# Two units of the FFN inside attention's last steps, expert 1's split moved to ScalarE and VectorE, zero rows issued by SyncE

## What is computed

```python
x = x + layernorm(attn(layernorm(x)))     # x: 2 batches x 2048 tokens x 256
x = x + layernorm(ffn(layernorm(x)))
# attn: 16 heads of 16, feature map elu(x)+1 on q (scaled) and k, gate = sigmoid(x Wg' + bg), per token
#   S = g * S + k v' ; y = q S ; output y Wo'
# ffn: one shared SwiGLU of width 512 for all tokens, and 8 experts of the same shape, top 2 per token:
swiglu = lambda x, w1, w2, w3: (silu(x @ w1) * (x @ w2)) @ w3
out = sum_e w[e] * swiglu(x, ew1[e], ew2[e], ew3[e]) + swiglu(x, sw1, sw2, sw3)
```

## Time and profile before

| | us |
|---|---|
| median of 3 runs | 824.59 |
| all runs | 824.56, 824.59, 828.3 |
| the profiled execution | 819.94 |
| its span, first to last instruction | 818.0 |
| TensorE busy | 725.9 (89%) |
| VectorE busy | 558.4 (68%) |
| GpSimd busy | 506.5 (62%) |
| ScalarE busy | 457.2 (56%) |
| mean granted TensorE clock | 0.964 |

### The profile page before, as it was taken

One profiled execution on the slowest core, in us unless ns is written; L12 is line 12 of the kernel. 1 busy time (PEld: TensorE's weight loads), 2 busy tenths in 40 slices (PEclk: granted clock), 3 DMA queues, 4 the chain that ended last, 5 costly groups with the idle time before them and its releaser, 6 DMA issues.

```text
span 818.0 us, 25456 instructions
## 1 busy us (share of the span) xinstructions
PE 725.9 (89%) x8863; PEld 607.8 (74%) x8863; DVE 558.4 (68%) x1126; ACT 457.2 (56%) x1023; POOL 506.5 (62%) x725
## 2 busy tenths in 40 slices
PE   4888989898999987287887999999999999999984
PEld 4667767786777776275776999999999986688873
DVE  4898897998998897478665444344444434358996
ACT  2655666575566654222444666656565657545443
POOL 4133334878687777578964888866666544316664
PEclk9999999999999998698999999999999999999998
DMA  7324332445344343956441111122222222227984
GB/s 256 95 76 128 107 93 80 138 126 152 101 144 119 107 132 102 311 165 195 120 128 51 46 54 40 55 72 79 87 86 82 70 60 66 85 89 208 187 177 89
DMA packets 57481, 93.25 MB, mean 114 GB/s; under 512 B 7216, under 2 KB 35760, under 8 KB 57360
## 3 DMA queue, kind: packets, MB, share of 16 engines
q1 hardware_dynamic: 40512, 60.66, 25.7%
q0 software_dynamic: 10672, 22.57, 10.2%
q10 hardware_dynamic: 6176, 8.40, 3.6%
HBM read 59.60 MB, written 32.01 MB: 112 GB/s over the span
## 4 chain that ended last, share of the span: by engine, by line
PE 40%; DVE 8%; POOL 7%; issue 5%; DMA 2%; ACT 2%; DVEq 0%; POOLq 0%; ACTq 0%; SPq 0%
PE bank L1294 22%; PE bank L1338 12%; PE bank L1314 3%; POOL xs_scratch L555 3%; PE bank L1278 2%; DVE wpart L1559 1%; POOL xs_scratch L588 1%; DVE bank L1655 1%; POOL W L1728 1%; DVE W L850 1%; DVE wtmp_p L1609 1%; DVE stc L1622 1%; DMA W<-gate_scratch 1%; DVE gl L1646 1%; ACT gh L1380 1%
## 5 line engine op out<-in xcount | busy, mean ns | idle before, releaser
L1294 PE MATMUL bank<-xh,W 128*128 128x256 f16 x1504 | 263.5, 277 | 21.2 <-DVE gl L1646 15.7
L1294 PE MATMUL bank<-xl,W 128*128 128x256 f16 x752 | 207.9, 277 | 1.4 <-issue 1.4
L1294 PEld LDWEIGHTS bank<-xh,W 128*128 (+1 forms) x1504 | 149.2, 99 | 45.9 <-issue 16.0
L1380 ACT ACTIVATE gh<-bank 128x512 f16<-128x512 f32 x103 | 61.3, 595 | 159.2 <-DVE bank L1655 146.4
L1338 PE MATMUL bank<-W,gh 128*128 (+1 forms) x824 | 138.0, 273 | 0.8 <-DVE gl L1646 0.8
L1743 POOL DMA_INDIRECT yt_scratch<-ysh,dest x71 | 76.2, 1073 | 97.7 <-ACT ysh L1435 58.5
L1646 DVE TENSOR_TENSOR gl<-bank,gh 128x512 f16<-128x512 f32 x103 | 71.0, 689 | 68.7 <-ACT gh L1380 67.4
L1338 PE MATMUL bank<-W,gl 128*128 (+1 forms) x412 | 112.3, 273 | 0.0
L555 POOL DMA_INDIRECT xs_scratch<-xn_all,posi x64 | 87.5, 1367 | 27.5 <-issue 15.2
L1655 DVE SCALAR_TENSOR_TENSOR bank<-sl,w_scale,bank 128x512 f32<-128x512 f32 x94 | 70.9, 755 | 48.7 <-PE bank L1294 40.2
L607 PE MATMUL bank<-xnT,wT 128*128 128x256 f32 x384 | 94.1, 397 | 2.3 <-ACT xnT L369 2.3
(11 more groups left out here) (205 smaller groups left out, 1386.4 us busy)
## 6 DMA issues: line engine op xcount, KB each, us to landing
W<-gate_scratch SPq DMA_DIRECT2D x64, 256.0 KB, 4.1
ysh<-yt_scratch SPq DMA_DIRECT2D x16, 512.0 KB, 4.7
xt<-xs_scratch SPq DMA_DIRECT2D x31, 260.0 KB
W<-in_L_ffn_ew_dram ACTq DMA_DIRECT2D x15, 512.0 KB, 3.8
W<-in_L_ffn_ew_dram SPq DMA_DIRECT2D x9, 512.0 KB, 8.7
x_in<-in_L_attn_x_dram SPq DMA_DIRECT2D x16, 256.0 KB, 3.7
out_dram<-x SPq DMA_DIRECT2D x16, 256.0 KB
xT_scratch<-xn2T SPq DMA_DIRECT2D x16, 256.0 KB
```

Of the source, the lines that this page charges most:

```text
L1294: last = mm(dst[n % 2][:, i * R:(i + 1) * R], W16[:, e, m, s, at:at + P], a[:, k, :], start=(k == 0 and s == 0 and a is x_h), stop=(k == K ...
L1380: act.activation(gh[t.u % 2][h][:, :], (pH1 if t.kind == "single" else pH2)[n % 2][:, :], ACT.Copy)\
```

## The change

Phase B's functions become generators that stop at `yield`; phase A's functions get `first_units`, a call that runs phase B up to its next `yield`, and the rest of phase B runs when phase A has ended. So units 0 and 1 are cut into pieces that stand at fixed places of iterations 17 and 18 on ScalarE, VectorE, TensorE and SyncE. What `tensor_b` waited for at its start is now waited for where it is needed.

- TensorE: behind all of iteration 17's work both halves of unit 0 and the first half of unit 1 (72 matmuls), behind iteration 18's (the router of step 15) the second half of unit 1; the two projections after phase A.
- Expert 1's three matrices are split as the shared ones are, by ScalarE (`scaled`, `high`) and VectorE (`low`) in iterations 17 and 18; `pool_b` begins with expert 2.
- The zero rows are eight plain DMAs of 128 rows by SyncE (`pad_experts`), each at a row read into a register, in phase B between the loads of units 3 and 4.
- `beside` is spread anew: searches for experts 2 and 3 in units 1 and 2, the table's last turn in unit 3, gap 2; the 15 searches for experts 4 to 8 in gaps 0 and 2 of units 4 to 11; the last scales in unit 12, gap 1. SHARE, the units at which SyncE shares maxima, goes from (0, 7) to (2, 11).
- The total of the counts goes to bank 6 (X1) in place of bank 7.

```diff
 def sync_a(sp, first_units):
             for i in range(FIRST, LAST):
+                if i == C + 1:
+                    first_units()
...
 def scalar_a(act, first_units):
                 on(share, i - 5)
+                if i == C + 1:
+                    first_units()
+                    for m in (3,):
+                        scaled(m)
+                        high(m)
+                if i == C + 2:
+                    first_units()
...
                 on(norm_x1, i - 3)
+                if i == C + 2:
+                    first_units()
                 on(turn_y, i - 2)
                 on(values, i - 1)
                 on(turn_xn2, i - 3)
                 on(lambda s: mask_q(s, 1), i - 1)
+                if i == C + 1:
+                    for m in (4, 5):
+                        scaled(m)
+                        high(m)
+                if C + 1 <= i <= C + 2:
+                    first_units()
...
 def pool_a(pool):
-            pool.wait_ge(s_pad, 1)
-            for e in range(E):
-                settle(pool)
-                pool.indirect_dma_start(xs_d[:, :], bass.IndirectOffsetOnAxis(ap=pad_row[:, e:e + 1], axis=0),
-                                        zrow[:, :], None).then_inc(s_padded, 16)
...
 def tensor_a(pe, first_units):
                 on(lambda s: scores(s, 0), i - 1)
-
-            pe.wait_ge(S["kT_ready"], C)
-            mm(X2[:, 0:E], ones[:, :], before[:, :, NB], start=True, stop=True).then_inc(s_total, 1)
+                if C + 1 <= i <= C + 2:
+                    first_units()
+
+            mm(X1[:, 0:E], ones[:, :], before[:, :, NB], start=True, stop=True).then_inc(s_total, 1)
...
 def vector_a(dve, first_units):
+                if i == C + 2:
+                    low(4)
+                    low(5)
+                    first_units()
                 on(stat_x1, i - 3)
+                if i == C + 2:
+                    first_units()
...
                 on(scan, i - 1)
+                if i == C + 1:
+                    first_units()
+                    low(3)
                 on(stat_o, i - 2)
...
 def sync_b(sp):
-        SHARE = (0, 7)
+        SHARE = (2, 11)
+            def pad_experts():
+                sp.wait_ge(s_pad, 1)
+                for e in range(E):
+                    row = sp.value_load(pad_row[0:1, e:e + 1], min_val=0, max_val=ZERO - P)
+                    sp.dma_start(xs_d[bass.ds(row, P), :], zrow[:, :]).then_inc(s_padded, 16)
+
+            sp.wait_ge(S["v_done"], C)
             load(units[0])
             load(units[1])
+            yield
             for u in range(ENDS):
                 if unit_at(u + 2):
                     load(units[u + 2])
+                if u == 1:
+                    pad_experts()
...
 def tensor_b(pe):
+            hidden(one, e_of[0], 0)
+            hidden(one, e_of[0], 1)
+            hidden(two, e_of[1], 0)
+            yield
+            hidden(two, e_of[1], 1)
+            yield
+            pe.wait_ge(S["ln_ready"], B * C)
+            project(one, e_of.pop(0))
+            pe.wait_ge(S["lg_ready"], C)
+            pe.wait_ge(S["slot_ready"], BIG)
+            pe.wait_ge(S["xn2T_ready"], C)
+            pe.wait_ge(s_counted, 1)
+            for u in range(2, NUNIT + 1):
...
 def scalar_b(act):
+            act.wait_ge(S["kT_ready"], C)
+            high_x(one)
+            high_x(two)
+            yield
             act.wait_ge(S["PV_done"], C * B)
             act.wait_ge(S["state_ready"], C * NU)
-            e_of = {0: expert_of(act, units[0])}
             load_matrices()
-            high_x(units[0])
-            for u in range(ENDS):
+            load_matrices()
+            yield
+            silu(one, 0, e_of[0])
+            act.wait_ge(w_low, 5)
+            act.wait_ge(experts_split, 1)
+            silu(one, 1, e_of[0])
+            high_g(one, 0)
+            yield
+            high_g(one, 1)
+            load_matrices()
+            yield
+            silu(two, 0, e_of[1])
+            high_x(units[2])
+            yield
+            high_g(two, 0)
+            silu(two, 1, e_of[1])
+            load_matrices()
+            high_g(two, 1)
+            e_of[2] = expert_of(act, units[2])
+            for u in range(2, ENDS):
...
 def vector_b(dve):
             def beside(u, gap):
-                turn = 3 * u + gap
+                turn, n = 3 * (u - 1) + gap - 1, 2 * (u - 4) + gap // 2
...
-                elif turn == TABLE + 4:
+                elif turn == 7:
                     rows_of_slots()
                     scales(link, dve, spread_b[0], 1)
-                elif turn < SCALES2 - 1:
-                    largest_of(*pieces[first_group + turn - REST])
-                    if turn == SCALES2 - 2:
-                        largest_of_group(2)
-                elif turn == SCALES2:
-                    scales(link, dve, spread_b[1], 2)
+                elif u == SHARE[1] + 1 and gap == 1:
+                    scales(link, dve, spread_b[1], 2)
+                elif gap != 1 and n < len(rest):
+                    largest_of(*rest[n])
+                    if n == len(rest) - 1:
+                        assert u == SHARE[1]
+                        largest_of_group(2)
...
+            low_x(one)
+            low_x(two)
+            yield
+            gated(one, 0, e_of[0])
+            yield
+            low_g(one, 0)
+            gated(one, 1, e_of[0])
+            low_g(one, 1)
+            gated(two, 0, e_of[1])
+            yield
+            low_x(units[2])
+            low_g(two, 0)
+            beside(1, 1)
+            gated(two, 1, e_of[1])
+            low_g(two, 1)
+            beside(1, 2)
...
 def pool_b(pool):
             def split(e):
-                done = 11 * (e - 1)
-                if e > 1:
-                    pool.wait_ge(experts_split, e - 1)
+                done = 11 * (e - HEAD)
+                pool.wait_ge(experts_split, e - 1)
...
-                for e in range(max(first, 1), end):
+                for e in range(max(first, HEAD), end):
...
             def _(sp):
-                sync_a(sp)
-                sync_b(sp)
+                late = sync_b(sp)
+                sync_a(sp, lambda: next(late))
+                finish(late)
```

More of the change, by code:

```diff
@@ L1342, in project @@
                 last.then_inc(T["y_done"], 1)
-            e_of = {}
-            for u in range(NUNIT + 1):
+            one, two = units[0:2]
+            e_of = {u: expert_of(pe, units[u]) for u in range(2)}
+            hidden(one, e_of[0], 0)
[11 more added lines that the diff above has]
+            for u in range(2, NUNIT + 1):
                 t, prev, following = unit_at(u), unit_at(u - 1), unit_at(u + 1)
@@ L1787, in sandwich_kernel, with finish @@
         phase_b.close()
+        def finish(late):
+            for _ in late:
+                pass
         with nc.Block() as block:
@@ L1807, in _ @@
             def _(dve):
[L1808 to L1809 removed]
+                late = vector_b(dve)
+                vector_a(dve, lambda: next(late))
+                finish(late)
             @block.tensor
             def _(pe):
[L1813 to L1814 removed]
+                late = tensor_b(pe)
+                tensor_a(pe, lambda: next(late))
+                finish(late)
 _INS = ['L0_attn_x', 'L0_attn_Wq', 'L0_attn_Wk', 'L0_attn_Wv', 'L0_attn_Wo', 'L0_attn_Wg', 'L0_attn_bg',
```

62 lines of the change are left out of this document (30 added, 32 removed).

## The result

| kernel | runs | median us | range | profiled execution | its span |
|---|---|---|---|---|---|
| before | 4 | 825.52 | 824.56 to 828.30 | 819.94 | 818.0 |
| changed | 4 | 804.39 | 795.86 to 806.99 | 806.99 | 805.2 |

The changed kernel is faster: ratio 0.972, 95% interval 0.964 to 0.980, about 21 us off the median. The forecast was 802.6 in a range of 797 to 813. That the two medians lie 1.8 us apart flatters it, for two reasons. And the profiled execution of before was a quick one, that of the changed kernel a slow one: only 12.95 us lie between them.

A forecast was written before the change was run, and what follows sets the result against it. GpSimd's scatters, zero rows and expert 1 split were taken to bound 346 to 397, a VectorE-ScalarE loop 397 to 454, then TensorE. Gains of 14.7 and 7.3 summed to 22.0 us off: median 802.6, range 797 to 813.

The forecast's parts named there:

- steps 1 and 2: Zero-row DMAs and expert 1's split leaving GpSimd free 24.9 us; then the slot table is late, 30.6 us behind attention.
- Step 3, D: Delay of the end of attention's last step by the early units' pieces: 2.0 us, with ends 0 and 9.
- The rival "clock": TensorE stays at 1.2 GHz among the early units, delaying attention's end by 9.1 us: 809.7 us; chance 0.13.
- Step 4: Zero rows on SyncE take some 10 us, from 348 to 358, and cost nothing within covers of 2 and 8 us.
- Step 5: First routed load: table at 378.5, reads 1.0, transfer 2.6; it lands at 382.2, 14.7 us earlier.
- Step 6: Searches spread over units 4 to 11 shorten the VectorE-ScalarE loop from 10.09 to 8.7-8.8 us: gain 7.3, between 2 and 9.
- The rival "searches": The VectorE-ScalarE loop isn't set by the searches' length, so the 7.3 us gain falls away: 809.9 us; chance 0.07.
- Step 7: GpSimd afterwards: expert 4's late split still serves unit 17 with 3 us cover; the tail from 765 on only moves.
- The rule weighed: Skill page on ScalarE tables: finish one function set before the next, a switch costs about 2.66 us; the sum has one load.
- The rival "tables": Two more table loads on ScalarE, 1.28 us each, before what VectorE waits for: 805.2 us; chance 0.06.

The follow-up runs named there:

- the kernel with zeros: The changed kernel with VectorE's three subtractions for expert 1's small parts replaced by writing zeros; 797.37 us in one run, the kernel before beside it 821.95.

## Why the prediction came out as it did, step by step

- **What bounds the kernel, steps 1 and 2**: right. GpSimd left the path and the table took its place, 30.4 us behind attention (30.6 predicted; that they agree to 0.2 is luck, since two traces of the old code differ by 0.9 here). Both removals were needed: with either back, the first rows come 4.6 to 5.4 later, not the 10.7 and 14.2 that were taken off GpSimd, since the table stands close behind. That is what costing the next thing in line was for.
- **Step 3, D**: 3.0 for 2.0, but by other pieces. The statistics were 3.6 late, for the 2.0 of the sum. Of the 1.6 that it lacked, the contention with GpSimd is most: the sum had VectorE's two subtractions "in its wait", which is true of VectorE, and didn't ask what they do to GpSimd's chain ahead of norm_o. It came 2.2 late for 0.4, of which the kernel with zeros gave back 1.3 to 1.5. TensorE's faster clock gave some back: transposes and router of step 15 took 0.66 and 1.06 us, where they had taken 1.12 and 1.88. The rival "clock" asked for half clock through all early units; the windows above have 1.00 from 332.5 on, where the sum had taken half clock for the first 3.3 us, and 0.50 only in the 2.6 us from 340.9.
- **Step 4**, zero rows on SyncE: nothing, as said. They went out from 353.91 to 362.8, and nobody waited. Each took 1.1 us with its read of a row number.
- **Step 5**: 4.37 us from table to transposes for 3.7, as the issue came 1.48 behind the table (1.0 taken, up to 1.7 kept) and the transfer took 2.85. 13.2 us earlier for 14.7.
- **Step 6**: 6.2 for 7.3. low_x to low_x took 8.8 to 9.1 us for 8.8. The same respacing in the kernel before gave 6.8 alone, by its trace. The rival "searches" is out.
- **Step 7 and the tail**: here the prediction failed. It had seen that expert 4's split comes late, and followed it to unit 17, the next user of the weights, where its cover held (TensorE's transposes there have no wait). It stopped there. The same queue holds every scatter of a routed row up to the last one, at 2.63 us each, and the tail's load waits for that. "The tail is the same code and only moves" was the wrong step: 3.7 us, which eight scatters put into the idle time gave back in full.
- **The rule weighed**: two table loads in all, the first ahead of attention and one of 1283 ns ahead of silu, none for the tanh of step 15 that comes after it (the tanh of step 14 still came ahead of the load, at 338.55). With the load moved further ahead both tanh stand behind a silu, and there are two loads again. The first silu started 0.02 us behind the load. The rival "tables" is out. Loading it earlier gained nothing at the end; the clock took it back.
- **The profiled time and the median**: 22.0 off a profiled 819.94 would have been 797.9; a profiled 806.99 came. 5.2 of the 9.1 us are the terms above, and 4.0 are attention, which started this part that much later, for a reason that stays open.

Both medians of the changed kernel lie in the range. The sign and the mechanism of the head were right, the tail's was not, and the sum was 5.2 too large; that the median came within 1.8 us of the forecast is luck.

## What to carry to other kernels

When work is moved or put off, follow the queue of every engine that it passes through to its last item, not only to the next user: a backlog that no unit notices can surface where the program drains. Before a wait is blamed, look at the engine that sets the pace: what it waited for, and what stood ahead of that transfer on its queue. And where runs differ by more than the effect, count from a common event just ahead of the change, after a look at whether that event has moved against what precedes it.

## What the runs showed of the hardware

- GpSimd and VectorE stop each other over SBUF. GpSimd's instructions on 2 to 4 columns took 0.65 us (beside low_x) and 1.17 us (beside a subtraction) instead of 0.19; with a memset in place of the subtraction the second took 0.19 again, while the first stayed. The other way, beside GpSimd's split, one of VectorE's products of 1x512 took 2.50 instead of 0.67, while its reductions of 1x512 kept their 0.67 and its operations on PSUM their 0.76. Another product of 1x512 kept its 0.70; beside it GpSimd's three casts took 3.91 instead of 3.38. The Trainium skill's page "SBUF — State Buffer" (section "Who interferes with whom") says that a VectorE instruction with two SBUF inputs and a GpSimd instruction that reads SBUF contend, since the second input comes through a read interface that the two engines share. By that rule the trace agrees. It isn't only that form, though: two tensor_scalar instructions of VectorE with one input took 0.69 and 1.08 instead of 0.17 beside the same split. It is a cost that no idle time shows: the instruction only looks longer.
- TensorE's granted clock fell from 2.4 to 1.2 GHz after a stretch in which it had been busy for 0.30 of 3.3 us in one kernel, and for 3.61 of 6.5 us in another. In a third it was busy for 3.61 of 6.8 us and the clock stayed, so that stretch alone doesn't decide it. In the second kernel an earlier finish of one engine met the slow stretch on the path.
- A tanh after silu needed no table load of its own.
